# Router logits of batches 0 to 5 by transposing transfers and 16-column bf16 products, in a fused attention and mixture-of-experts kernel

## The reference

```python
x = x + attention(layernorm(x), ctx)      # 8 batches of 256 tokens, 256 wide, 77 keys, 16 heads, two softmaxes
h = layernorm(x)                          # x2 in the kernel
probs = softmax(h @ gate_w.T)             # 8 experts: the router's logits
w, idx = top_k(probs, 2)
for e in range(8):                        # every token goes through two experts
    g, u = split(h @ gate_up[e].T)
    acc += combine[:, e] * (silu(g) * u @ down[e].T)
x = x + acc
```

## Time and profile before

| | |
|---|---|
| median of 3 runs | 545.44 us (543.28 to 546.12) |
| profiled execution, its time | 542.85 us |
| its span, first to last instruction | 541.1 us |
| mean granted TensorE clock | 0.952 |
| PE busy | 490.0 us (91%) |
| VectorE busy | 384.6 us (71%) |
| ScalarE busy | 339.7 us (63%) |
| GpSimd busy | 286.0 us (53%) |

### The profile page before, as it was taken

One profiled execution on the slowest core, in us unless ns is written; L12 is line 12 of the kernel. 1 busy time (PEld: TensorE's weight loads), 2 busy tenths in 40 slices (PEclk: granted clock), 3 DMA queues, 4 the chain that ended last, 5 costly groups with the idle time before them and its releaser, 6 DMA issues.

```text
span 541.1 us, 12094 instructions
## 1 busy us (share of the span) xinstructions
PE 490.0 (91%) x3720; PEld 364.2 (67%) x3735; DVE 384.6 (71%) x816; ACT 339.7 (63%) x643; POOL 286.0 (53%) x364
## 2 busy tenths in 40 slices
PE   4976989999998988797999999999999999999990
PEld 3845556766765655445778788888888888777650
DVE  5664368998978857794888888888766677666551
ACT  2333688988888886353776777776565556545530
POOL 7332646566546454244146576556656655554244
PEclk9978599999999999697999999999999999999997
DMA  8668676876776534434546877896665555643224
GB/s 258 179 180 257 192 199 184 263 198 191 255 194 190 182 113 147 146 108 132 163 106 137 181 178 153 184 167 165 100 92 95 90 82 94 99 79 61 30 30 50
DMA packets 87883, 79.89 MB, mean 148 GB/s; under 512 B 48456, under 2 KB 73832, under 8 KB 87688
## 3 DMA queue, kind: packets, MB, share of 16 engines
q1 hardware_dynamic: 75900, 62.93, 42.2%
q0 software_dynamic: 11856, 16.16, 18.6%
q10 hardware_dynamic: 68, 0.03, 0.0%
HBM read 49.08 MB, written 22.41 MB: 132 GB/s over the span
## 4 chain that ended last, share of the span: by engine, by line
PE 60%; DMA 11%; DVE 8%; issue 6%; ACT 6%; SPq 6%; POOL 3%; ACTq 0%; POOLq 0%; DVEq 0%
PE bank L1540 26%; PE bank L1559 13%; PE bank L1346 4%; PE bank L1332 3%; SPq L496 3%; PE bank L1297 2%; DMA q_parts<-WE 2%; PE bank L1571 2%; DMA FB<-w 2%; PE bank L1369 2%; PE bank L1355 2%; DMA FB<-x_parts,slot_tok 2%; PE bank L1313 2%; DVE FB L1224 2%; POOL out L749 1%
## 5 line engine op out<-in xcount | busy, mean ns | idle before, releaser
L1540 PE MATMUL bank<-FB,WE 128*128 128x0 bf16 x1440 | 190.2, 283 | 2.4 <-issue 1.6
L1540 PEld LDWEIGHTS bank<-FB,WE 128*128 x1440 | 138.7, 99 | 34.7 <-issue 4.1
L749 POOL DMA_INDIRECT out<-FB,slot_tok x60 | 100.2, 1669 | 87.5 <-DVE FB L1241 82.6
L943 ACT ACTIVATE FB<-FB 128x512 bf16<-128x512 f32 x120 | 75.6, 630 | 68.0 <-DVE FB L1220 64.6
L1224 DVE TENSOR_TENSOR FB<-FB 128x512 bf16<-128x512 f32 x120 | 83.3, 694 | 43.3 <-ACT FB L943 38.6
L1559 PE MATMUL bank<-FB,WE 128*128 128x0 bf16 x720 | 103.5, 280 | 2.9 <-DVE FB L1224 2.4
L1220 DVE TENSOR_TENSOR FB<-FB,bank 128x512 f32<-128x512 f32 x120 | 82.0, 683 | 26.7 <-ACT FB L937 21.5
L937 ACT ACTIVATE FB<-bank 128x512 f32<-128x512 f32 x120 | 70.7, 589 | 34.4 <-PE bank L1540 26.2
L740 POOL DMA_INDIRECT FB<-x_parts,slot_tok x60 | 63.7, 1062 | 52.5 <-DMA FB<-FB 31.6
L1559 PEld LDWEIGHTS bank<-FB,WE 128*128 x720 | 67.7, 98 | 21.8 <-issue 6.3
L656 POOL TENSOR_TENSOR WE<-FB,WE 128x256 bf16<-128x256 f32 x104 | 67.8, 678 | 21.1 <-ACT WE L780 21.1
(11 more groups left out here) (181 smaller groups left out, 612.1 us busy)
## 6 DMA issues: line engine op xcount, KB each, us to landing
FB<-w SPq DMA_DIRECT2D x26, 512.0 KB, 5.4
WE<-w SPq DMA_DIRECT2D x44, 256.0 KB
WE<-q_parts SPq DMA_DIRECT2D x32, 200.0 KB
WE<-x SPq DMA_DIRECT2D x16, 256.0 KB, 5.6
q_parts<-FB SPq DMA_DIRECT2D x32, 128.0 KB
x_parts<-WE SPq DMA_DIRECT2D x20, 128.0 KB, 3.9
out<-WE SPq DMA_DIRECT2D x20, 128.0 KB, 5.0
q_parts<-WE SPq DMA_DIRECT2D x16, 128.0 KB
```

Source lines behind the costliest of these rows:

```text
L749: pool.indirect_dma_start(out=out, out_offset=bass.IndirectOffsetOnAxis(ap=slot_tok[:, c:c + 1].bitcast(U32), axis=0), in_=result_tile(c), ...
L943: nc.scalar.activation(hT[k % 3][:, 0, :], hid[k % 2], ACT.Copy).then_inc(hi_ready, 1)
L1540: ins = nc.tensor.matmul(to, wf[:, bass.ds(at + o, P)], xgT[s % 2][:, 2 * part + kc, :].shape_from_register(long[s % 2]), start=(z == 0), ...
```

## The change

For tiles 0 to 11 (batches 0 to 5) PE no longer turns x2, and ScalarE no longer copies it. SP turns both bf16 parts of x2, which exist anyway for the gather, by one transposing transfer a tile into `x2T_parts`. PE multiplies the four turned 128x128 blocks (two parts by two halves of the width) with `gates`, where the gate's high part has 8 columns and its low part 8 more. VectorE adds the two groups of 8 columns and goes on as before. `N2`, `XH`, `XL`, `OX` and `LG`, `LC` have moved in the lists. `Z` is 12.

```diff
@@ buffers
+        gates = big(KC * 2 * E, BF16).rearrange("p (k s e) -> p k s e", k=KC, s=2)
+        sums = big(TPB * E).rearrange("p (t e) -> p t e", t=TPB)
+        x2T_parts = [v.rearrange("p (c n) -> p c n", c=2 * KC) for v in (x2T.bitcast(BF16), spare(2 * KC * P, BF16))]
@@ PE_PLAN
-            ("S", 9, 0), ("SC", 7, 1), ("PV", 1, 0), ("XT", 0, 3), ("LG", 0, -2), ("SC", 8, 1), ("SC", 9, 1), ("X2", 1, -2), ("S", 10, 0),
-            ("S", 11, 0), ("SC", 10, 1), ("Q", 0, 3), ("SC", 11, 1), ("OT", 1, -1), ("S", 12, 0), ("PV", 2, 0), ("S", 13, 0), ("PJ", 1, -1),
+            ("S", 9, 0), ("SC", 7, 1), ("PV", 1, 0), ("XT", 0, 3), ("SC", 8, 1), ("SC", 9, 1), ("X2", 1, -2), ("S", 10, 0),
+            ("S", 11, 0), ("SC", 10, 1), ("Q", 0, 3), ("SC", 11, 1), ("LG", 0, -2), ("OT", 1, -1), ("S", 12, 0), ("PV", 2, 0), ("S", 13, 0), ("PJ", 1, -1),
@@ ACT_PLAN
-            ("E", 1, 0), ("E", 2, 0), ("E", 3, 0), ("C2", 0, -2), ("XH", 0, -2), ("E", 4, 0), ("E", 5, 0), ("OC", 0, -1), ("E", 6, 0), ("E", 7, 0),
-            ("SQ", 0, -1), ("OS", 0, 0), ("H", 2, 0), ("E", 8, 0), ("E", 9, 0), ("OS", 1, 0), ("XC", 0, 3), ("H", 0, 1), ("XH", 1, -2), ("E", 10, 0),
+            ("E", 1, 0), ("E", 2, 0), ("E", 3, 0), ("C2", 0, -2), ("XH", 0, -2), ("E", 4, 0), ("XH", 1, -2), ("E", 5, 0), ("OC", 0, -1), ("E", 6, 0), ("E", 7, 0),
+            ("SQ", 0, -1), ("OS", 0, 0), ("H", 2, 0), ("E", 8, 0), ("E", 9, 0), ("OS", 1, 0), ("XC", 0, 3), ("H", 0, 1), ("E", 10, 0),
@@ DVE_PLAN
-            ("QL", 1, 2), ("MX", 0, 1), ("MX", 1, 1), ("DV", 0, -1), ("MX", 2, 1), ("MX", 3, 1), ("N2", 1, -2), ("LN", 0, 3), ("MX", 4, 1),
-            ("MX", 5, 1), ("DV", 1, -1), ("MX", 6, 1), ("MX", 7, 1), ("P1", 0, -1), ("LC", 0, -2), ("MX", 8, 1), ("MX", 9, 1), ("MX", 10, 1),
-            ("P2", 0, -1), ("MX", 11, 1), ("NEG", 0, 1), ("QL", 0, 3), ("XL", 0, -2), ("XL", 1, -2), ("P1", 1, -1), ("N2", 0, -1), ("P2", 1, -1),
+            ("QL", 1, 2), ("MX", 0, 1), ("MX", 1, 1), ("N2", 1, -2), ("DV", 0, -1), ("MX", 2, 1), ("MX", 3, 1), ("XL", 0, -2), ("LN", 0, 3), ("MX", 4, 1),
+            ("XL", 1, -2), ("MX", 5, 1), ("DV", 1, -1), ("MX", 6, 1), ("MX", 7, 1), ("P1", 0, -1), ("MX", 8, 1), ("MX", 9, 1), ("MX", 10, 1),
+            ("P2", 0, -1), ("MX", 11, 1), ("NEG", 0, 1), ("QL", 0, 3), ("LC", 0, -2), ("P1", 1, -1), ("N2", 0, -1), ("P2", 1, -1),
@@ SP_PLAN
-            ("QI", 1, 1), ("OX", 0, -3), ("OX", 1, -3), ("W", 2, 0), ("QOH", 0, 2), ("OO", 0, -2), ("XD", 0, -1), ("QOL", 0, 2), ("W", 0, 1),
-            ("OO", 1, -2), ("QOH", 1, 2), ("QOL", 1, 2), ("XA", 0, 4), ("W", 1, 1), ("QI", 0, 2), ("SH", 0, 1))
-        FIRST = {"XT": 3, ...
+            ("QI", 1, 1), ("W", 2, 0), ("QOH", 0, 2), ("OO", 0, -2), ("XD", 0, -1), ("QOL", 0, 2), ("W", 0, 1),
+            ("OO", 1, -2), ("OX", 0, -2), ("OX", 1, -2), ("QOH", 1, 2), ("QOL", 1, 2), ("XA", 0, 4), ("W", 1, 1), ("QI", 0, 2), ("SH", 0, 1))
+        FIRST = {"X2": B - 2, "C2": B - 2, "XT": 3, ...
@@ SP, kind OX
+                    if TPB * b + i < Z:
+                        if b > 0:
+                            sp.wait_ge(lg_mm, TPB * (b - 1) + i + 1)
+                        sp.dma_start(x2T_parts[i], x2s[:, i].rearrange("p s (k f) -> p (s k) f", k=KC), transpose=True).then_inc(x2_turned[i], 16)
                     sp.dma_start(xs[r:r + P, :], x2s[:, i].rearrange("p s n -> p (s n)")).then_inc(x2_out[i], 16)
@@ VectorE, once ahead of the loop
+            step(nc.vector.tensor_copy(gates[:, :, 0, :], gate_sb))
+            nc.vector.tensor_tensor(gates[:, :, 1, :], gate_sb, gates[:, :, 0, :], ALU.subtract).then_inc(gates_ready, 1)
@@ VectorE, kind LC
+                    if n < Z:
+                        halves = bank[bank_no("LG", n)][:, 0:2 * E].rearrange("p (s e) -> p e s", s=2)
+                        token_logits = sums[:, i, :]
+                        step(nc.vector.tensor_reduce(token_logits, halves, AX.X, ALU.add))
                     nc.vector.max(out=r_max[:, n, :], in_=token_logits).then_inc(top_ready, 1)
@@ PE
+            def gate_products(n, i):
+                if n == 0:
+                    pe.wait_ge(gates_ready, 1)
+                pe.wait_ge(x2_turned[i], 16 * (n // TPB + 1))
+                A = bank_for(bank_no("LG", n), lg_ready, n + 1)
+                for c in range(2 * KC):
+                    ins = nc.tensor.matmul(A[:, 0:2 * E], x2T_parts[i][:, c, :], gates[:, c % KC].rearrange("p s e -> p (s e)"),
+                                           start=(c == 0), stop=(c == 2 * KC - 1))
+                ins.then_inc(lg_mm, 1)
...
+                if kind == "LG" and n < Z:
+                    gate_products(n, i)
+                if kind == "LG" and n >= Z:
+                    product(x2T_of(n), x2T_ready, n - Z + 1, n, gate_sb, E, lg_mm, bank_no(kind, n), lg_ready)
```

More of the change, by code:

```diff
@@ L290, in moe_attention_kernel @@
         x2l_ready = sem("x2l_ready")
+        gates_ready = sem("gates_ready")
+        x2_turned = [sem(f"x2_turned{t}") for t in range(TPB)]
         x2t_mm = sem("x2t_mm")
@@ L366, in moe_attention_kernel @@
         SP_PLAN = (
-            ("QI", 1, 1), ("OX", 0, -3), ("OX", 1, -3), ("W", 2, 0), ("QOH", 0, 2), ("OO", 0, -2), ("XD", 0, -1), ("QOL", 0, 2), ("W", 0, 1),
-            ("OO", 1, -2), ("QOH", 1, 2), ("QOL", 1, 2), ("XA", 0, 4), ("W", 1, 1), ("QI", 0, 2), ("SH", 0, 1))
-        FIRST = {"XT": 3, "XC": 3, "Q": 3, "QH": 3, "QL": 2, "QOH": 2, "QOL": 2, "QI": 2, "LS": 4, "RS": 4, "LN": 4, "XA": 4, "SC": 1,
+            ("QI", 1, 1), ("W", 2, 0), ("QOH", 0, 2), ("OO", 0, -2), ("XD", 0, -1), ("QOL", 0, 2), ("W", 0, 1),
+            ("OO", 1, -2), ("OX", 0, -2), ("OX", 1, -2), ("QOH", 1, 2), ("QOL", 1, 2), ("XA", 0, 4), ("W", 1, 1), ("QI", 0, 2), ("SH", 0, 1))
+        FIRST = {"X2": B - 2, "C2": B - 2, "XT": 3, "XC": 3, "Q": 3, "QH": 3, "QL": 2, "QOH": 2, "QOL": 2, "QI": 2, "LS": 4, "RS": 4, "LN": 4, "XA": 4, "SC": 1,
                  "MX": 1, "W": 0}
@@ L828, in x2_hi @@
                     act.wait_ge(x2_out[i], 16 * b)
+                    act.wait_ge(x2_turned[i], 16 * min(b, Z // TPB))
                 nc.scalar.activation(x2s[:, i, 0, :], x2[:, i, :], ACT.Copy).then_inc(x2h_ready, 1)
             def x2T_copy(n):
-                act.wait_ge(x2t_mm, n + 1)
+                act.wait_ge(x2t_mm, n - Z + 1)
                 if n == TT - 1:
@@ L1102, in _ @@
                     if b > 0:
-                        dve.wait_ge(x2t_mm, TPB * (b - 1) + i + 1)
+                        if n - TPB >= Z:
+                            dve.wait_ge(x2t_mm, n - TPB - Z + 1)
                         dve.wait_ge(x2l_ready, TPB * (b - 1) + i + 1)
@@ L1356, in heads_to_tokens, with turned @@
                 ins.then_inc(dt_mm, 1)
-            def turned(src, src_sem, n, done, bank_no, taken_by):
+            def gate_products(n, i):
[7 more added lines that the diff above has]
+                ins.then_inc(lg_mm, 1)
+            def turned(src, src_sem, n, done, bank_no, taken_by, count):
                 pe.wait_ge(src_sem, n + 1)
-                A = bank_for(bank_no, taken_by, n + 1)
+                A = bank_for(bank_no, taken_by, count)
                 for k in range(KC):
@@ L1363, in turned, with product @@
                 ins.then_inc(done, 1)
-            def product(src, src_sem, n, weights, width, done, bank_no, taken_by):
-                pe.wait_ge(src_sem, n + 1)
+            def product(src, src_sem, count, n, weights, width, done, bank_no, taken_by):
+                pe.wait_ge(src_sem, count)
                 A = bank_for(bank_no, taken_by, n + 1)
@@ L1465, in _ @@
                 if kind == "OT":
-                    turned(o_sb[:, i, :], o_ready, n, otr_mm, bank_no(kind, n), oT_ready)
+                    turned(o_sb[:, i, :], o_ready, n, otr_mm, bank_no(kind, n), oT_ready, n + 1)
                 if kind == "PJ":
-                    product(oT, oT_ready, n, pj_sb, D, pj_mm, bank_no(kind, n), xm1_ready)
+                    product(oT, oT_ready, n + 1, n, pj_sb, D, pj_mm, bank_no(kind, n), xm1_ready)
                 if kind == "X2":
-                    turned(x2[:, i, :], x2_ready, n, x2t_mm, bank_no(kind, n), x2T_ready)
-                if kind == "LG":
-                    product(x2T_of(n), x2T_ready, n, gate_sb, E, lg_mm, bank_no(kind, n), lg_ready)
+                    turned(x2[:, i, :], x2_ready, n, x2t_mm, bank_no(kind, n), x2T_ready, n - Z + 1)
+                if kind == "LG" and n < Z:
+                    gate_products(n, i)
+                if kind == "LG" and n >= Z:
+                    product(x2T_of(n), x2T_ready, n - Z + 1, n, gate_sb, E, lg_mm, bank_no(kind, n), lg_ready)
             long = [nc.tensor.shape_register(n) for n in range(2)]
```

## The result

The changed kernel takes 568.19 us in the median of 4 runs (566.83 to 570.78) against 545.28 us (4 runs) before: 1.0447 times as long, 95% interval 1.0403 to 1.049. Forecast were 562 us, 552 to 574. The profiled execution took 570.78 us with a span of 569.0 us, 27.9 us above the span before.

The account below looks back on a forecast made before the run. PE was taken to set the pace, with VectorE 10% spare. Span 541.1 + 11.7 (bank-5 wait) + 5 (clock) + 0.5 (transfers) = 558.3; with 1.75 to the execution and 2.6 to the median, 562 us, range 552 to 574.

Parts of the forecast that it names:

- Steps 1 to 3: Attention loop: PE work falls 4 us in six passes, ScalarE loses 0.38 us a tile, VectorE gains a 0.25 us reduction.
- Step 4: VectorE's new order delays MX6 to MX8 up to 0.7 us, so PE's early saving is gone by SC11.
- Step 5: OT1 waits for LC0 to free bank 5, 2.75 us later in passes 2 to 4; 11.7 us in all.
- step 7: New transposing transfers on SP send the queries' outputs 3.2 us later; 0.5 us in all, bounds 0 and 1.5 a pass.
- small returns behind the hole: On PE after OT1's wait: LG1 gives back 0.1 us, small waits for ScalarE 0.1 to 0.5 a pass.
- Step 6: PE's clock halves behind three or four of five holes, at 1.4 us a fall: 5 us, bounds 0 and 15.
- (A): Stall at OT1 without falls of the clock: 557.6 us, or 556 with more given back; chance 0.18.
- (B): Every hole brings two long stretches of low clock, or the queries' late loading binds: 572 or 570 us; chance 0.13.
- (C): Faster: OT1 doesn't wait for LC0 and PE keeps 0.66 us a pass: 541.5 us; chance 0.04.
- (D): The wait at OT1 is right, but PE regains 0.6 us in each of six passes: 554 us; chance 0.07.

Follow-up runs that it names:

- experiment 2: Kernel before with only LG0 moved behind SC11 on PE and LC0 behind QL0 on VectorE, no transposing transfer: 564.89 us, 1.0306.
- experiment 1: Changed kernel with LG0 back between XT and SC8 on PE and LC0 back between P1 and MX8 on VectorE: 551.63 us, 1.0143.
- experiment 3: Changed kernel with LC0 directly behind MX11, ahead of NEG and QL0, on VectorE: 553.34 us, 1.0173.
- experiment 5: Changed kernel with LG0 of tiles 0 to 11 writing to bank 7 in place of 5, lists untouched: 551.89 us, 1.0143.
- experiment 4: Changed kernel with 20 bf16 matmuls that nothing reads, run on PE behind LG0 while it waits for bank 5: 560.09 us, 1.03.
- 6 and 7: Kernel before with N2, XH, XL and OX in changed places, with and without transposing transfers that nothing reads: 550.38 us with, 543.80 without.

## Why the prediction was right, and where its sizes were off

**Steps 1 to 3 (the work).** The new product steps by 0.10 us before the next group on PE where I took 0.25; the reduction takes 0.16 where I took 0.2. Neither mattered. With the step of 0.10, PE's work falls by 0.48 us a tile (0.22 + 0.36 - 0.10), 5.8 us in all, and not by 4.

**Step 4 (what PE saves is gone by SC11).** Right in passes 2 and 3: start to SC11 12.63 and 12.62 us, before 12.60 and 12.70. In passes 4 to 6 0.4 to 0.9 us were kept.

**Step 5 (bank 5), the main term.** Right in place, releaser and passes 2 to 6 (pass 7 had a hole of 0.88 us where none was expected), and shown: moving the two entries alone makes the loss (2), moving them back takes it away but for the transfers (1), shortening VectorE's list shortens the hole (3), another bank moves the wait to that bank's next user (5). Its size was low: holes of 2.4 to 3.2 us and passes of 23.7 to 26.6, where 2 to 2.6 and 22 to 24 stood. OT1 came 3.45 us later in pass 2 where 2.75 was the term, and over passes 2 to 6 15.1 us, where 13.5 (3 x 2.75 and 2 x 2.6) was. Two things stood in the way of a shorter one. From the start of MX11 to that of QL0 VectorE took 1.86 us in pass 2 where the earlier trace rows has 1.20: NEG's first instruction ran 0.69 us and not 0.20, its second 0.62 where pass 3 of the kernel before has 0.69. These are pass 3 before and, in the last line, QH0 on ScalarE in pass 2 after:

```profile
128.45 0.20 DVE L1037 TENSOR_SCALAR WE<-WE 128x64 bf16<-128x64 f32 x1
128.68 0.69 DVE L1038 SCALAR_TENSOR_TENSOR WE<-WE 128x64 bf16<-128x64 f32 x1
...
109.69 0.60 ACT L801 ACTIVATE FB<-bank 128x512 bf16<-128x512 f32 x1 [1.77 <-DMA q_parts<-WE]
```

QL0 needs QH0. That had waited 1.77 us for the write of q_parts and ended at 110.29, and QL0 began at 110.32, so a quick NEG alone would have gained nothing in pass 2. In pass 3 QH0 was done 0.43 us before QL0 began, and there NEG alone set the length; in pass 4 NEG was quick (0.20 and 0.23) and VectorE waited 0.87 us for QH0. That QH0 is late is step 7's late QOL1, with a waiter that I had not named: QH may not overwrite its buffer before that transfer is done. Why NEG ran long is not shown. In passes 2 to 4 of the changed kernel its instructions of 0.6 to 0.7 us run beside a TENSOR_TENSOR of GpSimd (in pass 2 from 108.79 on), and where they take 0.20 and 0.23, in pass 4, that one begins only as they end (160.00); no run separates the two. In experiment 2 the term came out at 2.76 us, almost the 2.75 of the sum, but with other parts: NEG took 0.45 us and QL0 waited 0.54 for QH0. The small returns behind the hole, 0.3 to 0.5 a pass, didn't show, since the clock had taken that stretch; in the filled run, with the clock at 1.00, they are there, 1.8 us in five passes (37.9 less 36.1).

**Step 6 (the clock), the term most off.** All five holes were followed by the lower level, not three or four, two shorter falls came in passes 5 and 6 where the kernel before has one, and the stretch from OT1 to the next start grew by 10.3 us in all where 5 stood, inside the bounds of 0 to 15. The filled run shows the price of the fall by itself: 10.46 - 7.33 = 3.1 us in pass 2, where it lasted from 112.0 to 118.8; and about 1.5 in passes 3 and 4 (8.87 and 8.97 us from OT1 to the next start), where it lasted some 3.4 us. Over passes 2 to 6 it is 12.1 us in the two traces (48.2 less 36.1), and in the medians 568.2 less 560.1, 8 us. The price of 1.4 read from the earlier trace rows was right for the short falls only.

**Step 7 (SP and the transfers).** Taken at 0.5 us, bounds 0 and 1.5 a pass. In the changed kernel it is hidden under the hole; once the hole is gone it is the term that remains: 1.2%, 6.6 us (6 and 7), near the upper bound. It isn't spread over the passes: it is the late queries at SC0 in passes 2 and 5, as step 7 had feared, and a fall of the clock behind the second. The landing of the turned parts was sized too low: 2.42 us by one row of the chain, whereas the trace after has 2.5, 4.2 and 6.3 us (min, median, max) from issue to landing. The estimate of 5.2 us worked out from the Trainium skill ("VectorE: DVE Perf Modes", section "The three transpose paths") was nearer, with 5.7 us from issue to use in experiment 1. The Trainium skill's advice to turn on TensorE where PSUM will do (same page, section "Rules for kernel authors") held here, since no place of the product found in four tries beat PE's own turns.

**The sum** 11.7 + 5 + 0.5 = 17.2 us stands against 27.9 in the spans: 15.1 - 1.9 = 13.2 for the hole net of what PE saved (11.7 had been that net, small returns and pass 7 included), 10.3 for the clock, the rest from outside these passes. What the 2.6 us behind the attention stage are was not settled; the first of the experts' products comes 24.7 us later than before (275.9 against 251.3) and PE's last instruction 27.8, so they lie with the experts.

**The rivals.** (A), no fall of the clock, is refuted; experiment 4 is what it would have looked like, 560 us where the rival had 556 to 558. (B), falls that last long or late transfers, was partly true: three of the five falls lasted over 6 us. (C) and (D) are refuted by the timeline.

## What to carry to other kernels

In an order written by hand, each buffer or PSUM bank that is handed on can make a hidden wait: before a producer is moved, look up who takes its bank next and how far down the reader's list its read stands. Moving one entry in each of two lists cost 3% here (some 17 us), about three times the 5.8 us of PE work that the new arithmetic saves. And a hole of 2 to 3 us on PE was paid twice here, once as it stands and once in the clock behind it, so the second part has to be in the sum from the start. Work moved from PE to transfers wasn't free here either: not by the load itself, which left passes 3 and 4 as they were, but by the transfers that came late behind it and the engine that waited for them. Before such a move, look for the next transfer in the queue that PE needs on time.

## What the runs showed of the hardware

- A hole of 2.4 to 3.2 us (in pass 5 in three pieces) with PE otherwise full went with half the clock in five cases of five, twice for 3.4 us and three times for 6.8. The fall began inside the hole in passes 5 and 6 (183.7 and 207.5), and 0.2 to 1.2 us behind it in the others. The five holes of 2.2 us in experiment 2 went with it too, at most 1.5 us behind. Filled for 2.3 us with matmuls that nothing reads, the granted clock was 1.00 in every microsecond from 95 to 225, where even the kernel before has a fall at 175, and the kernel went from 1.0447 to 1.03 of the time before by doing more. Holes of 0.97 and 0.98 us (experiment 3) and of 1.14 to 1.34 us (experiment 5) in passes 2 to 4 were followed by no fall.
- Two transposing transfers of 128 KB in 20 us raised the mean share of the transfer engines from 0.77 to 0.88 at nearly the same GB/s (225 and 234). 0.11 of 20 us is an estimated 1.1 us of all engines for each.
- One such transfer mostly took 1.2 to 1.3 us to issue on SP, some 2.0 to 2.3, at least twice the plain one of the same tile beside it (0.56 to 0.58 in pass 2).
